# A DLRM tower on one core: the steps of a chunk grouped by layer, two more split pairs, half of the low parts on VectorE

## What is computed

```python
# x: 512 x 32 x 16
for i in range(3):
    z = (x0[:, :, None, :] * h[:, None, :, :]).reshape(B, F * G, E)
    y = relu(einsum('oc,bce->boe', Ws[i], z) + bs[i])        # 128 outputs
    x_keep, h = halves of y for layers 0 and 1, y for layer 2
z = sum of the x_keep over the 16 components                  # 512 x 256
h = relu(concat([z, dense_ctx]) @ W_top1 + b_top1)            # 512
h = relu(h @ W_top2 + b_top2)                                 # 256
y = h @ W_top3                                                # 1
```

## Time and profile before

| what | us |
| --- | --- |
| three timed runs | 1859.66, 542.85, 543.13 |
| median of the three | 543.13 |
| the profiled execution's own time | 546.4 |
| its span, first to last instruction | 544.6 |
| TensorE busy in the span | 501.3 (92%) |
| VectorE busy | 379.8 (70%) |
| ScalarE busy | 196.1 (36%) |
| GpSimd busy | 358.2 (66%) |

### The profile page before, as it was taken

How to read it: one execution, slowest core, us unless ns; L and a number is a source line. 1 busy time by engine, 2 the same in 40 slices (tenths; PEclk the granted TensorE clock), 3 DMA queues, 4 the chain that set the end, 5 groups by cost and what they waited for, 6 DMA issues and landing times.

```text
span 544.6 us, 4268 instructions
## 1 busy us (share of the span) xinstructions
PE 501.3 (92%) x1446; PEld 273.1 (50%) x1446; DVE 379.8 (70%) x219; ACT 196.1 (36%) x253; POOL 358.2 (66%) x220
## 2 busy tenths in 40 slices
PE   0966769899999999999999999999999989899987
PEld 0622335355555555555545555555555554455555
DVE  1333964695959595959687786959595969867573
ACT  1210340434434443534253434334444424241242
POOL 5770347597969697887969696969697744715000
PEclk9897997999999999999999999999999999999999
DMA  7679599349998989797979797979798777350200
GB/s 230 131 164 255 150 243 233 105 110 250 219 247 184 250 182 238 167 235 160 228 158 231 166 227 161 221 166 243 159 220 199 171 196 159 89 110 9 76 0 0
DMA packets 33549, 94.50 MB, mean 174 GB/s; under 512 B 7844, under 2 KB 15012, under 8 KB 25080
## 3 DMA queue, kind: packets, MB, share of 16 engines
q1 hardware_dynamic: 27208, 91.87, 70.7%
q0 software_dynamic: 4096, 1.06, 1.7%
q10 hardware_dynamic: 2224, 1.31, 1.2%
HBM read 92.05 MB, written 2.10 MB: 173 GB/s over the span
## 4 chain that ended last, share of the span: by engine, by line
PE 75%; DVE 10%; issue 5%; DMA 4%; POOL 3%; ACT 2%; SPq 0%; DVEq 0%; ACTq 0%
PE acc L624 26%; PE acc L637 15%; PE spare L624 14%; PE x_bank L624 12%; DVE z L434 7%; PE x_bank L637 3%; POOL gathered L369 3%; PE spare L637 3%; DMA gathered<-in_table,rows_all 2%; DMA x_pair<-x_scratch 2%; DVE z L422 1%; DVE zl_parts L446 1%; DVE sum L451 1%; PE acc L642 1%; ACT h L534 1%
## 5 line engine op out<-in xcount | busy, mean ns | idle before, releaser
L382 POOL TENSOR_TENSOR z_low<-z,z_high 128x1024 fp32r<-128x1024 f32 x88 | 214.4, 2447 | 110.2 <-ACT z_high L520 109.4
L434 DVE TENSOR_TENSOR z<-h,x_pair 128x2048 f32<-128x2048 f32 (+1 forms) x65 | 144.8, 2248 | 115.8 <-ACT h L534 105.6
L624 PE MATMUL acc<-z,w_direct 128*128 128x512 f32 x384 | 175.0, 598 | 11.1 <-DVE z L434 11.1
L369 POOL DMA_INDIRECT gathered<-in_table,rows_all x128 | 143.6, 1122 | 33.3 <-issue 26.4
L520 ACT ACTIVATE z_high<-z 128x1024 fp32r<-128x1024 f32 x90 | 93.3, 1054 | 149.7 <-DVE z L434 127.7
L624 PEld LDWEIGHTS acc<-z,w_direct 128*128 128x128 f32 x384 | 72.9, 191 | 91.1 <-issue 71.9
L624 PE MATMUL spare<-z,w_direct 128*128 128x512 f32 x200 | 92.9, 603 | 11.2 <-DVE z L434 11.2
L624 PE MATMUL x_bank<-z,w_direct 128*128 128x512 f32 x200 | 89.9, 593 | 4.6 <-DVE z L434 4.6
L434 DVE TENSOR_TENSOR z<-h_odd,x_pair 128x2048 f32<-128x2048 f32 x32 | 72.3, 2278 | 8.1 <-ACT h_odd L534 8.1
L434 DVE TENSOR_TENSOR z<-h_even,x_pair 128x2048 f32<-128x2048 f32 (+1 forms) x33 | 72.3, 2213 | 5.2 <-ACT h_even L534 5.2
L624 PEld LDWEIGHTS spare<-z,w_direct 128*128 128x128 f32 x200 | 38.1, 193 | 55.6 <-issue 41.7
(11 more groups left out here) (144 smaller groups left out, 273.0 us busy)
## 6 DMA issues: line engine op xcount, KB each, us to landing
x_pair<-x_scratch SPq DMA_DIRECT2D x126, 512.0 KB, 7.2
x_rot<-x_scratch SPq DMA_DIRECT2D x60, 256.0 KB, 5.3
x_rep<-x_scratch SPq DMA_DIRECT2D x15, 256.0 KB, 5.1
w_direct<-in_W SPq DMA_DIRECT2D x2, 1024.0 KB, 8.6
gathered<-in_table,rows_all POOLq DMA_INDIRECT x128, 8.0
x_scratch<-gathered SPq DMA_DIRECT2D x32, 64.0 KB, 1.6
x_pair<-x_scratch ACTq DMA_DIRECT2D x2, 512.0 KB, 8.0
x_pair<-in_W_top SPq DMA_DIRECT2D x2, 512.0 KB
```

The source lines that it names most:

```text
L369: pool.indirect_dma_start(gathered[:, c % X_SLOTS, j, :], None, table, bass.IndirectOffsetOnAxis(ap=rows.bitcast(U32), axis=0),).then_inc( ...
L382: nc.gpsimd.tensor_tensor(z_low[:, slot_of(pair)], products_of(pair), z_high[:, slot_of(pair)].bitcast(F32), ALU.subtract).then_inc(low_po ...
L434: nc.vector.tensor_tensor(z[:, step.group % Z_SLOTS, first:end], h[:].unsqueeze(1).to_broadcast([P, end - first, N]), x_pair[:, chunk % 2, ...
L624: op = nc.tensor.matmul(bank_of(pair)[:], w_direct[:, first + i], products_of(pair)[:, i], start=i == 0 and pair is OPENS[pair.layer, pair ...
```

## The change

- `TURN` has another order: the steps of layer 1 (k 0, 1, 2) come first, then layer 0 of the next chunk, layer 1's k 3, then k 2 and 3 of layer 2 of the chunk before, and k 0 and 1 of layer 2 of this chunk. `FIRST`, `outputs()` and `SUM2` follow.
- `SPLIT` has six pairs in place of four, so eight pairs of 18 are split. Of the eight low parts VectorE makes four (`BY_VECTOR`) and GpSimd four.
- ScalarE copies `x_rep` to the PSUM bank `spare` (`copy_rep`) and `products0` reads it there. Layer 1 has only the bank `acc1`; `open_bank` waits accordingly.
- `x_pair` is laid out by i and then k, so each load writes four pieces of 512 columns per partition where it wrote one of 2048.
- In the start SP and ScalarE each issue four `x_pair` loads of chunk 0 at once. `x_first` is zeroed and has 128 rows, as has `sel`. `BUSY` is 30, and 22 transposes (`WARM`) stand ahead of steps (1, 0, 0) and (2, 0, 0).

```diff
-BUSY = 28
+BUSY, WARM = 30, 22
...
-TURN = ((1, 0), (2, 0), (1, 1), (2, 1), (0, 0), (1, 2), (1, 3), (2, 2), (2, 3))
...
+TURN = ((1, 0, 0), (1, 0, 1), (1, 0, 2), (0, 1, 0), (1, 0, 3), (2, -1, 2), (2, -1, 3), (2, 0, 0), (2, 0, 1))
...
-SPLIT = ((1, 0, 1), (1, 1, 1), (2, 1, 1), (2, 2, 1))
+SPLIT = ((1, 0, 1), (1, 1, 1), (1, 2, 1), (2, 0, 1), (2, 1, 1), (2, 2, 1))
...
+BY_VECTOR = ((0, 0, 1), (1, 1, 1), (2, 0, 1), (2, 1, 1))
...
     def load_half(eng, c, k, a):
...
-            eng.dma_start(x_pair[HALF * a:HALF * (a + 1), c % 2, GROUP * k:GROUP * (k + 1), :],
+            eng.dma_start(x_pair[HALF * a:HALF * (a + 1), c % 2, :, k, :],
...
-            for k in range(2):
+            for k in range(GROUPS):
                 load_half(sp, 0, k, 0)
             store_x(sp, 1)
-            for k in range(2, GROUPS):
-                load_pair(0, k)
...
             def products0(step):
                 dve.wait_ge(x0_here, X0_LOADS * 16 * step.chunk)
-                nc.vector.tensor_tensor(z[:, step.group % Z_SLOTS], x_rep[:].unsqueeze(1).to_broadcast([P, GROUP, N]),
+                dve.wait_ge(rep_made, step.chunk)
+                nc.vector.tensor_tensor(z[:, step.group % Z_SLOTS], spare[:].unsqueeze(1).to_broadcast([P, GROUP, N]),
...
+            def copy_rep(chunk):
+                act.wait_ge(x0_here, X0_LOADS * 16 * chunk)
...
+                nc.scalar.activation(spare[:], x_rep[:], ACT.Copy).then_inc(rep_made, 1)
...
-            for k in range(2):
+            for k in range(GROUPS):
                 load_half(act, 0, k, 1)
...
+                if n + 1 < len(PLAN) and PLAN[n + 1].layer == 0:
+                    copy_rep(PLAN[n + 1].chunk)
...
+            def keep_warm(bank, count):
+                for _ in range(count):
+                    nc.tensor.transpose(bank[:, 0:P], ident[:], ident[:])
...
             for n, step in enumerate(PLAN):
+                if step in HALVED:
+                    keep_warm(banks[step.layer][0], WARM)
```

More of the change, by code:

```diff
@@ L96, in plan @@
     start = step(0, 0, 0)
-    order = FIRST + [(layer, c + OF[layer], k) for c in range(2, CHUNKS + 1) for layer, k in TURN
-                     if c + OF[layer] < CHUNKS]
+    order = FIRST + [(layer, c + offset, k) for c in range(1, CHUNKS + 1) for layer, offset, k in TURN
+                     if c + offset < CHUNKS]
     return start, [step(*of) for of in order]
@@ L146 @@
 CLOSES = {(pair.layer, pair.chunk): pair for pair in ORDER}
-LAST1 = max((pair for step in PLAN for pair in step.by("pool") if step.layer < 2), key=lambda pair: pair.split)
-LAST_SLOT = max((pair for step in PLAN for pair in step.by("pool") if pair.split % PAIR_SLOTS == PAIR_SLOTS - 1),
+LAST1 = max((pair for step in PLAN for pair in step.by("vector", "pool") if step.layer < 2),
+            key=lambda pair: pair.split)
+LAST_SLOT = max((pair for step in PLAN for pair in step.by("vector", "pool") if pair.split % PAIR_SLOTS == 0),
                 key=lambda pair: pair.split)
@@ L179, in dlrm_tower @@
         gathered = sb("gathered", [P, X_SLOTS, GATHERS, EMBED])
-        x_pair = sb("x_pair", [P, 2, TILES, N])
+        x_pair = sb("x_pair", [P, 2, GROUP, GROUPS, N])
         x_rep = sb("x_rep", [P, N])
@@ L215, in dlrm_tower @@
         w_sym = z[:, 3].rearrange("p t n -> p (t n)")[:, 0:GROUP * P].rearrange("p (t o) -> p t o", o=P)
[L218 to L227, removed]
+        x_first = x_rot[:, 0, :]
+        sel = x_rot[:, 1:3].rearrange("p t n -> p (t n)")[:, 0:X0_LOADS * P].rearrange("p (t o) -> p t o", o=P)
+        free = x_pair[:, 0].rearrange("p i k n -> p (i k) n")
+        result = free[0:1, 0, :]
+        hid2 = free[:, 4:6, :]
+        wt1 = free[:, 6:8, :]
+        wt2 = flat(free[:, 8:10, :])
+        wd = free[0:COPIES * DENSE, 10, :]
+        wt1_high, wt1_low = z_high[:, 0], z_low[:, 0]
         wt2_high, wt2_low = [flat(w[:, 0:2 * N // P]) for w in (w_high, w_low)]
         sum01_high, sum01_low = zl_high[:], zl_parts[:]
-        sum2_high, sum2_low = z_high[:, 0, 0], z_low[:, 0, 0]
-        hid1_high, hid1_low = [parts[:, 1:3].rearrange("p s i n -> p (s i) n") for parts in (z_high, z_low)]
+        sum2_high, sum2_low = z_high[:, 1, 0], z_low[:, 1, 0]
+        hid1_high, hid1_low = [parts[:, 2:4].rearrange("p s i n -> p (s i) n") for parts in (z_high, z_low)]
         acc = [psum("acc0"), psum("acc1"), psum("acc2")]
@@ L435, in products @@
                                             h[:].unsqueeze(1).to_broadcast([P, end - first, N]),
-                                            x_pair[:, chunk % 2, GROUP * k + first:GROUP * k + end, :],
+                                            x_pair[:, chunk % 2, first:end, k, :],
                                             ALU.mult).then_inc(z_made if end == GROUP else first_made, 1)
@@ L609, in open_bank @@
             def open_bank(pair):
-                used = pair.chunk if pair.layer == 0 else pair.chunk - 1
+                used = pair.chunk - 1 if pair.layer == 2 else pair.chunk
                 if pair is OPENS[pair.layer, pair.chunk] and used > 0:
@@ L675, in _ @@
             turn_dense()
-            for _ in range(BUSY):
-                nc.tensor.transpose(acc[0][:, 0:P], ident[:], ident[:])
+            keep_warm(acc[0], BUSY)
             spread_first()
```

44 lines of the change are left out of this document (25 added, 19 removed).

## The result

| | runs | median us | ratio to before |
| --- | --- | --- | --- |
| before | 9 | 544.65 | |
| after | 9 | 539.30 | 0.990, 95% interval 0.9875 to 0.9922 |

The change is worth 5.4 us, 1.0%. Forecast were 533 us and a gain of 10 us. The profiled execution took 539.21 us with a span of 537.2, against 546.4 and 544.6 before.

The account below looks back on a forecast made before the run. It took a loop through TensorE, ScalarE and VectorE to bound the turn: 104.5 + 13 x 29.9 + 24.4 + 17.0 gave a span of 534.6 us, 10.0 less. Taken from the 543.13 median: 533 us, range 516 to 551.

Parts of the forecast that it names:

- the loop: Middle: TensorE, ScalarE, VectorE, then the product of (1, c+1, 3): 9.8 + 3.3 + 14.1 + 2.3 = 29.5 us.
- the turn: Middle, per chunk: the 29.5 us loop plus about 0.4 us of the square part meeting GpSimd, 29.9 us.
- the sum: Whole kernel: 104.5 + 13 x 29.9, then 24.4 of matmuls and 17.0 of dense tower; span 534.6 us.
- the start: First chunks: layer 2 begins at 50.5, 4.5 us sooner; (1, 2, 3) starts at 104.5, uncertain by some 4 us.
- held by the fuller matmuls: Start, 24 to 28 us: the granted clock, 0.59 before, should be held by the fuller matmuls.
- the tail: Behind (1, 15, 3): 10 D + 5 S + 0.27 = 24.4 us of direct and split pairs, then the dense tower.
- I take no change: x_pair loads: four pieces of 2 KB in place of one of 8 KB cost no more time.
- from span to median: End of the sum: 10 us off 543.13, the median of the runs shown, gives 533 us.
- TensorE as the bound: Rival, middle: TensorE never waits, turns of 28.48 and 513 us; chance 0.16.
- The whole wait each turn: Rival, middle: a VectorE low part waits a whole GpSimd subtraction, 2.4 us; turns of 31.9, 561 us; chance 0.07.
- random collisions: Rival, middle: two-operand VectorE instructions meet GpSimd at random, 1.5 us per turn; turns of 31.0, 548 us; chance 0.13.
- loads: Rival, middle: smaller x_pair pieces make loads the bound; turns of 31.3 or 34.5, about 553 or 597 us; chance 0.04.

Follow-up runs that it names:

- the first experiment: The changed kernel with ScalarE's output of layer 0 one step later, so the z_high of step (2, c, 0) stands ahead of it: 525.54 us, ratio 0.964.
- the second: The changed kernel with the low part of pair (2, c, 0, i=1) made by GpSimd in place of VectorE: 527.94 us, ratio 0.969.
- The run with one step less: The changed kernel with the split pair that closes layer 1 of the last chunk multiplied one step after its products, not two: 537.38 us, ratio 0.987.

## Why the prediction was right in the middle and wrong in size, point by point

**Right: the loop.** Its four terms in after, from the rows above and TensorE's timeline, are 9.63, 3.20, 14.18 and 2.33 us, 29.34, against 9.8, 3.3, 14.1 and 2.3 in the text. VectorE's wait for `z_high` was to be 2 us and is 1.77; it stands where it was to stand, behind layer 0's output. That this is the bound was argued then and is shown by the first experiment; the second agrees. Right also: the product from PSUM at 2.28, the layer-0 product no longer waiting, TensorE without a hole in layer 1 of chunk 0 after the first loads.

**Mis-sized: the turn,** 29.33 and not 29.9. Half of this is the port wait. The square part was to lose 0.4 us per turn and loses 0.11 (0.85 for 0.74). The 0.4 us falls on the low part at 289.12 (1.62 for 1.22), which stands behind the product that TensorE waits for, off the loop. The other half is the first two terms, 9.63 for 9.8 and 3.20 for 3.3. In 12 turns that makes 6.8 us. The thirteenth, without a layer-0 step, takes 27.3 us and not 29.9, because one split pair slips out of it into the tail: 2.6 us more. Together the sum had 9.4 us too much.

**Wrong: the start,** (1, 2, 3) at 104.5. It is at 113.25, 8.75 us later. This is the step that failed, the term of the sum that was set too small by most:

- Layer 2 begins at 52.76, not 50.5: layer 0's loads of chunk 1 end at 46.2, not 44.
- The clock. I had it "held by the fuller matmuls", and the stretch 24 to 28 us came out so (1.00 now, 0.59 in the earlier trace rows), though no run shows that the fuller matmuls did it. But my own times left TensorE idle ahead of layer 2 and again ahead of (1, 1, 3), and I priced those idle times at their length only. They cost 1.9 and 3.0 us more, as the run with more transposes shows.
- The square part of that first turn takes 2.92 us in place of 0.74, since GpSimd's subtraction starts at 74.06, just ahead of it. The prediction takes the steady turn's collisions for those of the start. This part and the first are read from the trace of after; no run takes them away.

```profile
74.09 2.92 DVE L459 SCALAR_TENSOR_TENSOR zl_parts<-zl_high,signs,zl_full 128x512 fp32r<-128x512 f32 x1
```

The three are 2.3 + 4.9 + 2.2 = 9.4; the first turn, the clock left aside, is shorter by 0.6 than laid out and gives back the rest.

**Wrong: the tail,** 24.4 us of matmuls. It is 27.7 (492.5 to 520.2). The last turn has no layer-0 step, and the sum overlooks both things that follow from it. Split pairs are multiplied two steps behind, so one more than I counted, (1, 15, 1), stands behind (1, 15, 3): six and not five, 1.4 us, which the turn ahead gave up. And the pair that closes layer 1 stands behind a direct pair of layer 2, so that VectorE stands 6.07 us for the last h. I summed TensorE's work as if it could not wait there; it does, for the other 1.9 us. The run with one step less gets 1.9 us back.

**Wrong: the layout "I take no change".** It is worth 3.3 us to the change's side, by the start alone. My landing time for the `x_pair` loads, 39 us, was worked out with the rate of the old pieces; the last product that waits for them starts at 38.28 in after and at 40.45 with the old pieces.

**Wrong: from span to median.** The sum gave a span of 534.6 and the span is 537.2, 2.6 us off, because the errors above (-9.4, +8.75, +3.3) nearly cancel. That is luck: a turn summed too long hid a start and a tail summed too short. The other 3.7 us are the step from the span to the median: I put 10.0 us off the median of three runs, 543.13, while nine runs give 544.65, and after's runs lie 2.1 us above their span. The profiled execution of before was itself 1.8 us above the nine-run median, so that 7.4 us between the two spans are 5.4 between the medians.

**The rivals.** TensorE as the bound, at 28.48 per turn and 513 us, did not come about, but it is what one moved output makes of it: 28.46. The whole wait each turn, 31.9 and 561 us, is about what the kernel does without the copy, 31.37 and 569.8, though there the square part waits and not a low part. Neither random collisions nor loads set a turn: 29.33 each time, with the old layout too.

## What to carry to other kernels

When engines run fixed lists, sum the work of each, then lay out the longest loop through several of them, and look in it for an instruction that waits ahead of one that doesn't have to: here one such place was worth 14 us, and the two new split pairs nothing until it was gone. Price an idle time of TensorE at its length and, where the granted clock falls behind it, at that clock too, and try useless matmuls to fill it. Work out start and end as carefully as the turn, with their own orders and collisions; here they were 12 us longer than summed.

## What the runs showed of the hardware

- In the run that reads `x_rep` in SBUF, VectorE's product with two SBUF inputs started 0.12 us ahead of GpSimd's subtraction and took its 2.28 us; the subtraction took 4.42 and VectorE's next instruction 2.89 in place of 0.85. In the kernel before, where the subtraction was first, the product itself took 3.03.
- Idle times of 6.93 and 3.63 us were followed by a granted clock of 0.50, where the eight records took up to 6.66 us; behind one of 2.64 us, in the run that reads `x_rep` in SBUF, they took 3.70. The length alone doesn't decide it: in the kernel before with the new start, eight such records behind an idle time of 2.14 us took 5.40.

```profile
95.54 5.40 PE L625 MATMUL acc<-z,w_direct 128*128 128x512 f32 x8 [2.14 <-DVE z L435]
```

- Loads of 512 KB to 64 partitions, beside gathers and with the DMA engines full, moved 206 to 331 GB/s in pieces of 2 KB and 231 to 238 in pieces of 8 KB, from 24 to 36 us of the start.
- On two of the four chips of the experiments the kernel before took 18 and 19 us more. In the traces there, of the changed kernel without its 44 transposes ahead of (1, 0, 0) and (2, 0, 0), ScalarE's copy of the spread `x_rep` came 9 and 22 us later than in after, and layer 2 began 16 and 17 us later.
